# A graph attention layer of 4096 nodes: its columns in groups of six, one and one blocks instead of four, three and one

## The reference

```python
h = jnp.maximum(_layernorm(x, axis=-1), 0.0)          # x: 4096 x 128
H = h @ W_fc + b_fc                                   # 4096 x 128
scores = (H @ w_att[:d])[:, None] + (H @ w_att[d:])[None, :] + b_att
scores = jnp.where(adj > 0, scores, NEG_INF)          # adj: 4096 x 4096 int32, 64 MiB
out = x + softmax(scores, axis=1) @ H
```

## Time and profile before

| | us |
|---|---|
| median of 3 runs | 189.28 (188.98 to 189.49) |
| the profiled execution, its time | 189.04 |
| its span in the trace | 187.3 |
| outside the span | 1.74 |

### The profile page before, as it was taken

One profiled execution on the slowest core, in us unless ns is written; L12 is line 12 of the kernel. 1 busy time (PEld: TensorE's weight loads), 2 busy tenths in 40 slices (PEclk: granted clock), 3 DMA queues, 4 the chain that ended last, 5 costly groups with the idle time before them and its releaser, 6 DMA issues.

```text
span 187.3 us, 2525 instructions
## 1 busy us (share of the span) xinstructions
PE 164.5 (88%) x866; PEld 112.3 (60%) x866; DVE 144.4 (77%) x407; ACT 32.6 (17%) x90; POOL 7.1 (4%) x28
## 2 busy tenths in 40 slices
PE   0449827999999999999999989999999999999950
PEld 0326606666666766666657657577766566776740
DVE  0899869899969887777799996479995644699552
ACT  2346256055068100000040000000000004000010
POOL 2102130000030000000000000000000000000000
PEclk9999995899999999999999999999999999999997
DMA  6999999999999999999999999999999999999202
GB/s 182 385 423 427 422 422 422 420 418 423 418 423 420 420 422 423 422 422 408 419 417 417 417 417 416 420 419 415 414 419 413 420 426 423 416 396 349 81 3 58
DMA packets 13268, 71.61 MB, mean 382 GB/s; under 512 B 1604, under 2 KB 2374, under 8 KB 8134
## 3 DMA queue, kind: packets, MB, share of 16 engines
q1 hardware_dynamic: 12528, 71.18, 92.6%
q10 hardware_dynamic: 726, 0.27, 0.6%
HBM read 69.34 MB, written 2.10 MB: 381 GB/s over the span
## 4 chain that ended last, share of the span: by engine, by line
PE 43%; DMA 22%; DVE 17%; issue 12%; ACT 3%; POOL 2%; DVEq 0%; POOLq 0%
DMA ring<-adj 22%; PE bank L705 16%; PE bank L711 15%; DVE mask L403 8%; PE bank L729 5%; PE bank L753 5%; ACT weighted L325 2%; DVE low L425 2%; DVE mask L412 1%; PE bank L743 1%; DVE stats L419 1%; DVE high_bits L484 1%; DVE x_sb L507 1%; DVE x_sb L515 0%; DVE weighted L592 0%
## 5 line engine op out<-in xcount | busy, mean ns | idle before, releaser
L403 DVE TENSOR_SCALAR mask<-ring 128x2048 fp32r<-128x2048 int32 (+1 forms) x66 | 71.8, 1095 | 24.3 <-DMA ring<-adj 13.8
L705 PE MATMUL bank<-mask,high 128*128 128x512 f32 x256 | 82.1, 424 | 7.9 <-ACT high L331 7.1
L711 PE MATMUL bank<-mask,low 128*128 128x512 f32 x256 | 75.9, 399 | 0.0
L705 PEld LDWEIGHTS bank<-mask,high 128*128 128x128 f32 x256 | 47.3, 197 | 31.2 <-issue 12.6
L711 PEld LDWEIGHTS bank<-mask,low 128*128 128x128 f32 x256 | 49.4, 193 | 11.3
L729 PE MATMUL bank<-mask,w_cols 128*32 128x512 bf16 x256 | 22.8, 393 | 0.9 <-POOL w_cols L305 0.9
L359 ACT COPY sums_T<-bank 128x512 f32<-128x512 f32 x8 | 4.2, 597 | 110.7 <-PE bank L711 110.7
L729 PEld LDWEIGHTS bank<-mask,w_cols 128*32 128x32 bf16 x256 | 4.3, 94 | 13.7 <-issue 12.4
L337 ACT ACTIVATE relu<-x_sb,neg_mean 128x128 f32<-128x128 f32 x32 | 9.7, 394 | 8.8 <-DVEq L439 8.8
L325 ACT ACTIVATE weighted<-relu,w_over_std 128x128 f32<-128x128 f32 x32 | 10.1, 392 | 2.1 <-DVE w_over_std L476 2.1
L515 DVE SCALAR_TENSOR_TENSOR x_sb<-bank,inv_den,x_sb 128x128 f32<-128x128 f32 x32 | 9.0, 344 | 1.7 <-PE bank L753 1.0
(11 more groups left out here) (79 smaller groups left out, 52.0 us busy)
## 6 DMA issues: line engine op xcount, KB each, us to landing
ring<-adj SPq DMA_DIRECT2D x39, 1024.0 KB, 21.2
ring<-adj SPq DMA_DIRECT2D x32, 768.0 KB, 18.0
out<-x_sb SPq DMA_DIRECT2D x7, 256.0 KB, 13.0
x_sb<-x SPq DMA_DIRECT2D x1, 1024.0 KB, 13.6
ring<-adj SPq DMA_DIRECT2D x4, 256.0 KB, 21.9
x_sb<-x SPq DMA_DIRECT2D x1, 768.0 KB, 5.2
x_sb<-x SPq DMA_DIRECT2D x1, 256.0 KB, 3.5
out<-x_sb ACTq DMA_DIRECT2D x2, 64.0 KB, 1.6
```

The costliest lines, as they stand in the source:

```text
L403: nc.vector.tensor_scalar(mask[:, n % MASKS, 0:cols], ring[:, n % RING, 0:cols], 0.0, None, ALU.is_gt).then_inc(masks_ready, 1)
L705: nc.tensor.matmul(bank[:, b, :], high[:, t, :], mask[:, n % MASKS, cols], start=(t == 0), stop=False)
L711: last = nc.tensor.matmul(bank[:, b, :], low[:, t, :], mask[:, n % MASKS, cols], start=False, stop=(t == T - 1))
```

## The change

The groups become 6, 1 and 1 blocks wide. Group 0 still has one unit for each tile j, now 1.5 MiB; groups 1 and 2 both have units of four tiles, 1 MiB. That makes 32 + 8 + 8 = 48 units, 24 pairs. One transfer now brings a pair (3 MiB in group 0, 24 KiB in a row for each partition; 2 MiB in groups 1 and 2, 16 KiB), into a ring of three slots; pair p is issued once both masks of pair p-3 are made. Pair 0 comes as two transfers with a semaphore each, with the first two pieces of x before and between them, the third piece of x after pair 2, and the last pair as one of 1 MiB and four of 256 KiB.

The denominators of six blocks go into one bank (now bank 6): blocks 0 to 3 of both tiles of a pair take the four strips as before, blocks 4 and 5 of the first tile take strips 0 and 1, those of the second tile strips 2 and 3, with the weight columns shifted by four, and `inverse_of` adds the two halves. `sums_T` for all eight blocks now lies where `relu` was, so its first copy waits for the running row sum, which moves from group 1 into group 0 (units 17 to 24). The products of blocks 0 to 5 stand behind the pairs 16 to 19 (two, two, one, one), the product of block 6 behind pair 21, and they use banks 1 to 4. The results are made behind the masks of units 35, 37, ... 45 and 46. The small inputs of the launch come in two transfers instead of five, and the masks that stood inside the reciprocal square root of the later stages are made outside it. The general path changes where it used `relu`.

```diff
-GROUPS = [(0, 4), (4, 3), (7, 1)]
-RING = 10
+GROUPS = [(0, 6), (6, 1), (7, 1)]
+WIDEST = 6
+RING = 3
...
-        ring = sb("ring", [P, RING, 4 * BLOCK], I32)
-        mask = sb("mask", [P, MASKS, 4 * BLOCK], F32R)
+        ring = sb("ring", [P, RING, 2 * WIDEST * BLOCK], I32)
+        mask = sb("mask", [P, MASKS, WIDEST * BLOCK], F32R)
...
+            half = WIDEST * BLOCK
+            for i in range(2):
+                tiles = slice(*STAGES[i])
+                sp.dma_start(x_sb[:, tiles, :], x_v[:, tiles, :]).then_inc(x_landed[i], 16)
+                sp.dma_start(ring[:, 0, i * half:(i + 1) * half], adj_g[0][0][:, i * half:(i + 1) * half]).then_inc(first_landed[i], 16)
+            for pair in range(1, LAST_PAIR):
+                g, t0, step = UNITS[2 * pair]
+                cols = 2 * step * GROUPS[g][1] * BLOCK
+                if pair >= RING:
+                    sp.wait_ge(masks_ready, 2 * (pair - RING) + 2)
+                sp.dma_start(ring[:, pair % RING, 0:cols], adj_g[g][t0 // (2 * step)]).then_inc(pair_landed[pair % RING], 16)
+                if pair == 2:
+                    tiles = slice(*STAGES[2])
+                    sp.dma_start(x_sb[:, tiles, :], x_v[:, tiles, :]).then_inc(x_landed[2], 16)
+            sp.wait_ge(masks_ready, 2 * (LAST_PAIR - RING) + 2)
+            sp.dma_start(ring[:, LAST_PAIR % RING, 0:4 * BLOCK], adj_g[2][3][:, 0:4 * BLOCK]).then_inc(next_to_last_landed, 16)
+            for i in range(PER):
+                cols = slice((PER + i) * BLOCK, (PER + i + 1) * BLOCK)
+                sp.dma_start(ring[:, LAST_PAIR % RING, cols], adj_g[2][3][:, cols]).then_inc(last_landed[i], 16)
...
+            def unit_landed(n):
+                pair = n // 2
+                if pair == 0:
+                    dve.wait_ge(first_landed[n], 16)
+                elif n == LAST - 1:
+                    dve.wait_ge(next_to_last_landed, 16)
+                else:
+                    dve.wait_ge(pair_landed[pair % RING], 16 * (pair // RING + (pair % RING > 0)))
...
+            def first_mask(b):
+                cols = slice(b * BLOCK, (b + 1) * BLOCK)
+                if b == 0:
+                    unit_landed(0)
+                last = nc.vector.tensor_scalar(mask[:, 0, cols], ring[:, 0, cols], 0.0, None, ALU.is_gt)
...
                     if k == 0 and i < 6:
-                        stats_of(STAGES[1][0] + i)
+                        first_mask(i)
...
+            def denominator(n, t, at, q, v, start, stop):
+                return nc.tensor.matmul(bank[32 * q:32 * q + 32, DEN_BANK, :], w_cols[:, t, 4 - 4 * v:36 - 4 * v],
+                                        mask_16[:, n % MASKS, at * BLOCK:(at + 1) * BLOCK, 1],
+                                        start=start, stop=stop, tile_position=(0, 32 * q))
...
+                    for b in range(4):
+                        denominator(first, t, b, b, 0, first == 0, False)
+                    for b in range(4, 6):
+                        denominator(first, t, b, b - 4, 1, False, False)
+                    for b in range(4, 6):
+                        denominator(first + 1, t + 1, b, b - 2, 1, False, False)
+                    for b in range(4):
+                        last = denominator(first + 1, t + 1, b, b, 0, False, last_pair)
...
                 if g == 1:
                     if local == 0:
                         pe.wait_ge(constants_ready, 1)
+                        pe.wait_ge(sums_copied, 6)
                         den_columns(0)
-                    if local in (12, 14, 16, 18):
-                        products(0, (local - 12) // 2)
+                    if local in (0, 2):
+                        products(0, local)
+                        products(0, local + 1)
+                    if local == 4:
+                        products(0, 4)
+                    if local == 6:
+                        products(0, 5)
                 if g == 2:
                     if local == 0:
                         den_columns(1)
+                    if local == 2:
                         products(1, 0)
-                        products(1, 1)
-                    if local == 4:
-                        products(1, 2)
```

More of the change, by code:

```diff
@@ L207, in gnn_kernel @@
         out_stored = sem("out_stored")
+        gen_x_landed = sem("gen_x_landed")
         gen_d_ready = sem("gen_d_ready")
@@ L355, in _ @@
                 for b in range(width):
[L356 to L359, removed]
+                    act.wait_ge(sums_done, b0 + b + 1)
+                    if g == 0 and b == 0:
+                        act.wait_ge(row_sum_ready, 1)
+                    nc.scalar.copy(sums_T[:, b0 + b, :], bank[:, SUMS_BANK[g] + b, :]).then_inc(sums_copied, 1)
                 if g < LAST_GROUP:
@@ L529, in _ @@
             scores(0, last)
-            mask_quarter(0, 0)
+            for t in range(4, 6):
+                last = stats_of(t)
             row_weights(0)
-            for i in range(1, 4):
-                mask_quarter(0, i)
+            for t in range(6, 8):
+                last = stats_of(t)
             split(0)
@@ L536, in _ @@
             mask_unit(1)
-            for t in range(10, 16):
+            split(2)
+            for t in range(8, 16):
                 last = stats_of(t)
-            split(2)
             moments(1, last)
+            mask_unit(2)
             for t in range(4, 16):
@@ L543, in _ @@
             scores(1, last)
-            mask_unit(4)
+            mask_unit(3)
             row_weights(1)
[L546 to L550, removed]
+            for n in range(4, 7):
+                split(n - 1)
+                mask_unit(n)
             for n in range(7, 9):
@@ L578, in _ @@
                     link(nc.vector.tensor_reduce(b_logits[:], ab_prod, AX_X, ALU.add))
-                if n == 22:
-                    link(nc.vector.tensor_tensor(product[:], v_rows[:, 0, :], v_rows[:, 0, :], ALU.mult))
-                    link(nc.vector.tensor_reduce(v_square[:], product[:], AX_X, ALU.add))
-                if n in range(23, 23 + CHUNKS):
-                    rows = x_sb[:, (n - 23) * PER:(n - 22) * PER, :]
-                    link(nc.vector.tensor_tensor(rows, rows, b_row.unsqueeze(1).to_broadcast([P, PER, D]), ALU.add))
@@ L620, in _ @@
-                if g == 2:
-                    if local == 3:
-                        inverse_of(1)
-                    if local in (4, 5, 6):
-                        result_of(1, local - 4, results_ready)
+                if n == 20:
+                    link(nc.vector.tensor_tensor(product, v_rows[:, 0, :], v_rows[:, 0, :], ALU.mult))
+                    link(nc.vector.tensor_reduce(v_square[:], product, AX_X, ALU.add))
+                if n in range(24, 24 + CHUNKS):
+                    rows = x_sb[:, (n - 24) * PER:(n - 23) * PER, :]
+                    link(nc.vector.tensor_tensor(rows, rows, b_row.unsqueeze(1).to_broadcast([P, PER, D]), ALU.add))
@@ L642, in _ @@
                 nc.vector.tensor_scalar(d_logit[:], d_raw[:], b_logits[:, 1:2], None, ALU.add).then_inc(gen_d_ready, 1)
+                dve.wait_ge(gen_x_landed, 16)
+                for t in range(T):
+                    last = nc.vector.tensor_scalar(relu[:, t, :], relu[:, t, :], neg_mean[:, t:t + 1], 0.0, ALU.add, ALU.max)
+                link(last)
                 for t in range(T):
@@ L721, in denominators @@
                 if g == 0:
-                    pe.wait_ge(w_cols_ready, STAGE_OF[UNITS[first][1]] + 1)
-                if first == 0:
-                    pe.wait_ge(lines_ready, 1)
-                for n in (first, first + 1):
-                    _, t0, step = UNITS[n]
-                    for q in range(width * step):
-                        t = t0 + q // width
-                        last = nc.tensor.matmul(bank[32 * q:32 * q + 32, DEN_BANK, :], w_cols[:, t, :],
-                                                mask_16[:, n % MASKS, q * BLOCK:(q + 1) * BLOCK, 1],
-                                                start=(n == FIRST[g]), stop=(n == FIRST[g] + COUNT[g] - 1),
-                                                tile_position=(0, 32 * q))
+                    t = UNITS[first][1]
@@ L733, in denominators @@
+                    for b in range(4):
+                        last = denominator(first + 1, t + 1, b, b, 0, False, last_pair)
+                else:
+                    for n in (first, first + 1):
+                        for i in range(PER):
+                            last = denominator(n, UNITS[n][1] + i, i, i, 0, n == FIRST[g], last_pair and n == first + 1)
                 last.then_inc(pairs_done, 1)
             def den_columns(g):
-                width = GROUPS[g][1]
-                rows = 32 * width if width > 1 else P
```

291 lines of the change are left out of this document (142 added, 149 removed).

## The result

The changed kernel takes 189.99 us (median of 16 runs) against 189.21 before (16 runs). One of the 16 runs before took 215.38 us; the ratio leaves it out, and the median isn't moved by it. The span of the profiled execution is 188.3 us, 1.0 longer than before.

The account below looks back on a forecast made before the run. Bound: the transfer stream until about unit 41, then PE. PE's end 4.0 us later, less 0.8 for longer rows, makes 3.2; on the profiled 189.04 that is 192.2, and 0.24 to the median gives 192.4 us, range 190.2 to 195.0.

Parts of the forecast that it names:

- Two bounds in turn: Whole kernel before the change: the transfer stream bounds it until about unit 41, then PE work alone.
- Rate of longer rows: Wide-group transfers: 24 KiB rows gain 0.8 us, between 0 and 1.6, at the most 2.3.
- Longer rows bring most of it back: Rival on the wide pairs: at 430 GB/s pair 15 lands 2.3 us sooner, time 191.0; chance 0.17.
- the fit of groups 0 and 1: Transfers before the change: two unit times give 430 GB/s for the bytes and 0.05 us for each transfer.
- Landing of pair 15 with the old rows: Last wide pair: at 421 GB/s it lands whole at 130.4 us.
- The wide pair on PE: Wide group: PE needs 6.56 us for a pair, third denominator round 0.28, against 7.46 of stream.
- The mask before it: Before pair 15 on PE: the mask of unit 30 takes 1.84 us.
- The narrow end: Behind pair 15: 43.7 us of PE work against 40 us of stream, so PE is the bound and ends at 182.5.
- Covered costs: Narrow end: bank copies, DVE's stop for the inverse and the slots cost nothing, covered by PE's own lateness.
- my line on a full bandwidth row: Sign of being right: the stream's bandwidth row stays full until slice 36; a hole would point to the slots.
- The start: First pairs: the first mask's later wait, perhaps 3 us, is hidden because fifteen wide pairs give back 13 us.
- PE's short stops before the wide pairs: Wide group: about 0.9 us each; a rival (slots or clock, chance 0.15) had the clock fall, giving 195 to 198.

Follow-up runs that it names:

- e5: Changed kernel, each wide pair still one 3 MiB transfer, but its two units apart in HBM, giving two 12 KiB rows per partition: 190.95 us, ratio 1.0081.
- e1: Changed kernel, each wide pair from pair 1 on as two 1.5 MiB transfers with 12 KiB rows, DVE waiting for both: 191.12 us, ratio 1.0105.
- e7: Changed kernel, each wide pair as three 1 MiB transfers with 8 KiB rows, DVE waiting for the whole pair: 191.95 us, ratio 1.0152.
- e3: Changed kernel, wide pairs as two transfers with 12 KiB rows and a semaphore for each unit, so DVE waits only for its half: 189.92 us, ratio 1.0046.
- e6: Changed kernel, only the last two wide pairs as two 12 KiB-row transfers with a semaphore for each unit, the others whole: 189.39 us, ratio 1.0008.
- e4: Changed kernel, products of blocks 0 to 6 doing one of their four parts, so those results are incomplete: 186.42 us, ratio 0.9857.
- b2: Kernel before the change, group 0 brought by pairs of units (16 KiB rows) up to unit 27, units 28 to 31 one by one: 188.17 us, ratio 0.9947.
- b1: Kernel before the change, all of group 0 brought by pairs of units (2 MiB, 16 KiB rows) into neighbouring slots: 189.16 us, ratio 0.9992.
- e2: Changed kernel, each wide pair as two 1.5 MiB transfers, each over 64 partitions with 24 KiB rows: 309.25 us, ratio 1.636.

## Why the prediction was right in sign and wrong in size

The kernels with wide groups side by side, all read in the same way from their traces (in those that land whole pairs, unit 31 lands with unit 30; the last column is the median):

| kernel | row, KiB | unit 31 lands | PE starts narrow | last denominators | time |
|---|---|---|---|---|---|
| changed | 24 | 127.85 | 136.12 | 178.91 | 189.99 |
| e5 | 12 | 128.82 | 137.10 | 179.89 | 190.95 |
| e1 | 12 | 128.92 | 137.21 | 180.00 | 191.12 |
| e7 | 8 | 129.84 | 138.12 | 180.91 | 191.95 |
| e3 | 12, by units | 130.10 | 136.29 | 179.08 | 189.92 |
| e6 | 24, last two pairs 12, by units | 128.00 | 135.16 | 177.95 | 189.39 |

- **Two bounds in turn: right for the changed kernel.** From the start of the narrow pairs to the last denominators all six have the same 42.79 us. Nothing but the moment at which PE enters them moves the end, and e4 shows that it is PE's work that fills them. For the kernel before, the reading was too simple: its chain of waits rests on transfers up to 108 us, but PE lost only 0.87 us in two stops (1.9 with smaller gaps, by b2), the first of them at 91.92, where the prediction had PE caught up by 65 us, when the chain came to rest on transfers. The 6.8 us of saved work did turn into idle time, as forecast, because PE can't start a wide pair before it has landed.
- **The step that failed: "Rate of longer rows".** It took 0.8 us, between 0 and 1.6, with 2.3 as the most. e7 against the changed kernel measures 1.99 at the landing and 1.96 in the time. The mechanism was named, and the rival "Longer rows bring most of it back", which took 2.3, came closer; the term was mis-sized. I had held the fit of groups 0 and 1 against group 2's 419 GB/s with 8 KiB rows and halved it. The runs bear out the fit's side and more: per row on a DMA engine (16 engines, 8 rows of each transfer apiece) 460.9 ns for 12 KiB and 912.7 for 24, a line with 9.1 ns for each row and 37.65 for each KiB. It gives 235.0 for 6 KiB (1.878 us for 8 rows before: 234.8), 310.3 for 8 (e7: 310.5) and 611.5 for 16 (b1: 612.1). Without rows it would be 435 GB/s and not the 430 that I had from two numbers which lie close together. The Trainium skill's "DMA: Bandwidth & Descriptors", Specifications, has 435 GB/s as its ceiling; the line's limit agrees, though the most that a run here reaches is 431. Of the 3.8 us that the prediction worked out from that ceiling, 24 KiB rows brought 2.0.
- **Landing of pair 15 with the old rows: right within 0.6.** 130.4 was the sum, e7 has 129.84.
- **The wide pair on PE:** 6.56 forecast, 6.45 measured; the third round costs 0.22 and not 0.28. **The mask before it:** 1.84 forecast, 1.82 measured.
- **The narrow end:** 43.7 forecast, 43.36 measured (42.79 and the last 0.57).
- **Covered costs:** the slots did hold the stream up, against my line on a full bandwidth row (slices 31 and 33, 141.2 to 145.9 and 150.6 to 155.3 us): pairs 20 and 21 are issued only at 144.02 and 148.57, each right behind the second mask of the pair three before it. It cost nothing, as argued: PE has no idle time behind 129.67. DVE kept its promise too, but not for my reason. The 23% that it had free on the page are not in the narrow end, where it is full; what covers it is PE's own lateness, 3.4 us of it.
- **The start** was hidden as said, and PE's short stops before the wide pairs (0.35 before pair 15) left the granted clock at full.

So of the 2.4 us between 192.4 and 189.99, 1.2 are the rows. The rest are small terms that all erred to the same side: 0.55 in the landing, 0.1 in the wide pair, 0.3 in the narrow end. The remaining 0.2 or so lie between traces and medians: the sum added 0.24 to come from the profiled execution to the median, but the changed kernel's profiled execution (190.18) is 0.19 above its median. What made the landing 0.55 earlier is not shown, beyond that e7 already had 0.45 of it when its pair 10 landed (92.63, where 421 GB/s from unit 32's 92.46 gives 93.08); so most of it stems from the first half, where the prediction put the new order of x and the small inputs at nothing. Without the rows, e7 is slower than before by 2.7 where the sum had 4.0.

Still open: why group 2 of the kernel before lands at 2.50 us a unit when 8 KiB rows take 2.48 elsewhere, and why the first narrow pair lands 5.9 us behind pair 15 (133.79 - 127.85) when 16 KiB rows need 4.90; it does so in all these kernels but e3, where unit 31 is the one that comes 1.0 late. This costs nothing in the changed kernel and is what PE came to wait for in e6 and e3. Fixed slots for the narrow pairs, to fill the holes in the stream, were not tried, as PE hides them.

## What to carry to other kernels

Where the stream of transfers sets the pace, lay the data out so that a partition's row in a transfer is long, and take the price of a row from a line through two lengths that lie far apart. But let the last transfers before another engine becomes the bound land in small pieces, because there the whole of a large one is waiting time: b2 does both and is the fastest. Work that an engine no longer has to do counts only where that engine is the bound; here 6.8 us less of PE work bought nothing, because the work was saved ahead of a landing that PE has to wait for, and the 43 us of work behind it began later. And before you call a stretch bound by transfers because the chain of waits rests on them, add up what the engine beside them really waited there: it was 0.87 us in two stops, 1.9 with the smaller gaps, and no more was to be had from a faster stream.

## What the runs showed of the hardware

- A DMA engine's time for a row fits a line of about 9 ns and 37.65 ns for each KiB (rows of 6 to 24 KiB, HBM to SBUF, one core, transfers queued back to back). The size of a transfer made no difference: 7.375 us for a pair in two transfers of 1.5 MiB (e1), 7.38 in one of 3 MiB (e5).
- Transfers over 64 of the 128 partitions, one behind the other, ran at half the rate: 210 GB/s in e2 against 431, with the DMA engines shown busy throughout.
